# The last step of a two-part kernel, 512 tokens, is made into two steps of 256

## What is computed

```python
def _mlp(x, W1, b1, W2, b2):
    h = jax.nn.gelu(x @ W1 + b1, approximate=False)
    return h @ W2 + b2
...
def attn(x, ...):                      # x: layernorm of the input
    q, k, v = _mlp(x, W1q, ...), _mlp(x, W1k, ...), _mlp(x, W1v, ...)
    scores = jnp.einsum('bid,bjd->bij', q, k) / scale
    scores = scores * jnp.tril(jnp.ones((T, T)))
    out = jnp.einsum('bij,bjd->bid', scores, v)
    mu = jnp.mean(out, axis=-1, keepdims=True)
    var = jnp.mean(jnp.square(out - mu), axis=-1, keepdims=True)
    return (out - mu) * jax.lax.rsqrt(var + LN_EPS) * ln_w + ln_b
...
def ffn(x, tile_sigs, W, b):           # x: layernorm of the sum so far
    idx = jnp.argmax(jnp.einsum('sp,tp->st', pe, jnp.sign(tile_sigs)), axis=-1)
    y_all = jnp.einsum('bsd,tod->bsto', x, W) + b
    return the row idx[s] of y_all[b, s]
...
x = x + attn(_layernorm(x), ...)
x = x + ffn(_layernorm(x), ...)
```

## Time and profile before

| what | value |
|---|---|
| median of 3 runs | 318.12 us (317.26 to 319.13) |
| span of the profiled execution, first to last instruction | 313.3 us |
| what lies around the span, from the median | 4.8 us |
| PE busy | 288.0 us, 92% |
| DVE, ACT, POOL busy | 236.7, 188.7, 177.3 us |
| mean granted TensorE clock | 0.982 of full |

### The profile page before, as it was taken

How to read it: one execution, slowest core, us unless ns; L and a number is a source line. 1 busy time by engine, 2 the same in 40 slices (tenths; PEclk the granted TensorE clock), 3 DMA queues, 4 the chain that set the end, 5 groups by cost and what they waited for, 6 DMA issues and landing times.

```text
span 313.3 us, 5485 instructions
## 1 busy us (share of the span) xinstructions
PE 288.0 (92%) x1806; PEld 255.3 (81%) x1806; DVE 236.7 (76%) x539; ACT 188.7 (60%) x380; POOL 177.3 (57%) x238
## 2 busy tenths in 40 slices
PE   8799999998999999999999999999999975594994
PEld 6578888997898888889788989898988965583983
DVE  5858878899889979968986896798568677272556
ACT  2636677676676876676778667779664452372400
POOL 6882813360684559475646626584564857276551
PEclk9999999999999999999999999999999999599899
DMA  7909970011022110311121000250132331942111
GB/s 232 221 2 301 358 224 16 0 52 51 0 74 67 36 71 2 86 53 37 58 78 62 9 2 20 82 170 20 70 123 87 110 135 69 259 130 80 32 42 34
DMA packets 24209, 27.83 MB, mean 89 GB/s; under 512 B 4659, under 2 KB 22068, under 8 KB 24118
## 3 DMA queue, kind: packets, MB, share of 16 engines
q1 hardware_dynamic: 15910, 13.68, 15.1%
q0 software_dynamic: 3296, 8.64, 8.0%
q10 hardware_dynamic: 4976, 5.16, 5.1%
HBM read 13.95 MB, written 14.44 MB: 91 GB/s over the span
## 4 chain that ended last, share of the span: by engine, by line
PE 69%; DVE 9%; issue 6%; DMA 4%; ACT 4%; SPq 3%; POOL 2%; another core or an unknown queue 2%; ACTq 0%; POOLq 0%; DVEq 0%
PE ring L491 39%; PE o_ps L491 10%; PE s_ps L491 6%; DMA w_stage<-w2v 3%; PE w_ps L491 3%; ACT xn L982 3%; SPq L454 2%; PE ring L519 2%; PE sc_ps L604 2%; POOL out_dram L1743 1%; DVE xres L1219 1%; PE sc_ps L602 1%; PE w_ps L647 1%; DVE xres L1450 1%
## 5 line engine op out<-in xcount | busy, mean ns | idle before, releaser
L491 PE MATMUL ring<-xnT,w_sp 128*128 128x512 f32 x288 | 73.5, 399 | 5.1 <-DVE hT L1152 3.2
L491 PEld LDWEIGHTS ring<-xnT,w_sp 128*128 128x128 f32 x288 | 51.9, 189 | 17.4 <-DVE hT L1152 4.0
L882 ACT ACTIVATE ring<-ring,b_cols 128x512 f32<-128x512 f32 x48 | 31.7, 660 | 29.5 <-PE ring L491 28.2
L491 PE MATMUL ring<-hT,w_sp 128*128 128x512 f32 x192 | 46.4, 396 | 0.0
L1152 DVE TENSOR_TENSOR hT<-ring,hT 128x512 fp32r<-128x512 f32 x48 | 32.3, 680 | 14.3 <-ACT hT L885 12.7
L491 PEld LDWEIGHTS ring<-hT,w_sp 128*128 128x128 f32 x192 | 35.4, 188 | 8.1 <-DVE hT L1152 0.2
L1678 POOL DMA_INDIRECT sorted_rows<-xres,slot_i x30 | 31.2, 1041 | 8.5 <-issue 6.5
L1743 POOL DMA_INDIRECT out_dram<-slot_rows x22 | 21.9, 996 | 18.6 <-DVE slot_rows L1436 13.6
L1644 POOL TENSOR_TENSOR vtok<-v,vtok 128x512 fp32r<-128x512 f32 x14 | 17.9, 1289 | 25.4 <-ACT vtok L902 25.4
L885 ACT CAST hT<-ring 128x512 fp32r<-128x512 f32 x48 | 28.2, 587 | 1.5
L1219 DVE SCALAR_TENSOR_TENSOR xres<-cen,rs,xres 128x256 f32<-128x256 f32 x32 | 23.9, 761 | 3.6 <-issue 3.6
(11 more groups left out here) (245 smaller groups left out, 682.0 us busy)
## 6 DMA issues: line engine op xcount, KB each, us to landing
sorted_rows<-blank ACTq DMA_DIRECT2D x1, 5032.0 KB, 20.5
xt<-x SPq DMA_DIRECT2D x7, 512.0 KB, 3.6
slot_rows<-sorted_rows SPq DMA_DIRECT2D x22, 136.0 KB, 3.6
w_stage<-tile_w SPq DMA_DIRECT2D x8, 256.0 KB, 2.8
h<-sorted_rows SPq DMA_DIRECT2D x15, 136.0 KB, 3.0
xt<-x SPq DMA_DIRECT2D x2, 256.0 KB, 3.0
hT<-position_table POOLq DMA_DIRECT2D x1, 512.0 KB, 9.3
sorted_rows<-xres,slot_i POOLq DMA_INDIRECT x30
```

Of the source, the lines that this page charges most:

```text
L491: last = te.matmul(o, lhs[k][a], rhs[k][c], start=start and k == 0 and i == 0, stop=stop and k == n - 1 and i == 2, skip_group_check=check)
L882: nc.scalar.activation(full, ring[(2 + m) % 3][:, :], ACT.Gelu, bias=b1c[:, m // 2, m % 2:m % 2 + 1]).then_inc(gelu, 1)
```

## The change

Steps 0 to 6 keep 512 tokens. The former step 7 becomes step 7 (`FULL`) and step 8 (`LAST`) of 256 tokens each. Step 7 is a normal step of two chunks: it updates the state, and its back stands in the front of step 8. Step 8 holds the two dense chunks; no row of it is sorted. The sorted rows of step 7 are sent while step 8's front runs. `place(m)` moves the turning of the dense pair to position 13 (`LATER`), ahead of pair 13, and the dense products are put between pairs 13 to 17. Low parts of v are made by VectorE in both half steps, where GpSimd did it for full steps.

```diff
-STEPS = NB * PER
+FULL = NB * PER - 1
+NCH = (CH,) * FULL + (CH // 2, CH // 2)
+STEPS = len(NCH)
 LAST = STEPS - 1
+BASE = [sum(NCH[:s]) for s in range(STEPS + 1)]
...
-AMID, INNER, MIDDLE = 1, 5, 8
+AMID, INNER, MIDDLE, LATER = 1, 7, 8, 13
...
+        def place(m):
+            return m if m < LATER else LATER if m == PAIRS else m + 1
...
+            HALF_ROWS = H_ROWS + 6 * GT // ROW
...
             for n in range(H_ROWS, SLOTS):
                 if n == FIRST:
-                    sp.wait_ge(fill, FILLS * LAST + 14)
+                    rows_there(FULL)
+                if n == EARLY:
                     rows_there(LAST)
-                if n == EARLY:
-                    rows_there(STEPS)
+                if n == HALF_ROWS:
+                    sp.wait_ge(fill, FILLS * STEPS)
...
+            def last_scores():
+
+                te.wait_ge(q_lo, 2 * STEPS)
+                te.wait_ge(k_lo, 2 * STEPS)
+                te.wait_ge(xb_lo, AMID + INNER)
+                for j in range(2):
+                    mm3(sc_bank[j].rearrange("p (c n) -> p c n", n=P),
...
+            s = FULL
             front_transposes(LAST)
             back_state(s, 0)
...
+            front_h(LAST, (0, 1), False)
+            pair_transposes(3)
             back_scores(s, 0)
...
+            front_h(LAST, (2,), False)
             back_chunk(s, 1)
...
+            front_h(LAST, (3,), False)
             pair_products(3)
             pair_transposes(4)
+            front_h(LAST, (4, 5), False)
+            pair_products(4)
+            pair_transposes(5)
+            front_qk(LAST, 0, False)
+            pair_products(5)
+            pair_transposes(6)
+            front_qk(LAST, 1, False)
+            pair_products(6)
             front_v(LAST, False)
...
+            for m in range(LATER, PAIRS):
+                pair_transposes(m)
+                dense_products((m - LATER) // 4, (m - LATER) % 4)
+                pair_products(m)
+            for i in range(PAIRS - LATER, NT):
+                dense_products(i // 4, i % 4)
...
+            chunk_rest(FULL, 0)
+            chunk_rest(FULL, 1)
+            xnT_rest(LAST)
+            half_v_rest(FULL, 0)
+            half_v_rest(FULL, 1)
+            scores_rest(FULL)
+            state_rest(FULL, 0)
+            out_centred(FULL, 0)
```

More of the change, by code:

```diff
@@ L258, in mk_seq_kernel @@
         wide = carve(2 * CLASSES * NT * NJ)
+        x_late = [wide[:, i * 2 * C:i * 2 * C + 2 * C].rearrange("p (c d) -> p c d", c=2) for i in range(2)]
         chosen = wide.rearrange("p (a j t) -> p a j t", a=2 * CLASSES, t=NT)
@@ L437, in _ @@
             load_tile(1)
-            for s in range(LAST):
+            for s in range(STEPS - 3):
                 if s == 3:
@@ L551, in front_h @@
                             te.wait_ge(xnT_lo, 2 * s + 1 + k)
-                        last = mm3(ring[(2 + m) % 3][:, :], [wpair(m // 2, k, m % 2 * P, m % 2 * P + P)],
-                                   [[xnT[:, a, k, :] for a in range(2)]], start=k == 0, stop=k == KC - 1)
+                        last = mm3(ring[(2 + m) % 3][:, 0:width(s)], [wpair(m // 2, k, m % 2 * P, m % 2 * P + P)],
+                                   [[xnT[:, a, k, 0:width(s)] for a in range(2)]], start=k == 0, stop=k == KC - 1)
                     last.then_inc(fill, 1)
@@ L782, in pair_products @@
                 last.then_inc(y_ps, 1)
-            for s in range(LAST - 1):
+            for s in range(FULL - 1):
                 front_transposes(s + 1)
@@ L1101, in _ @@
             pair_norm(9)
-            for m in range(MIDDLE + 1, PAIRS + 1):
+            pair_rounded(9)
+            pair_norm(10)
+            pair_rounded(10)
+            pair_norm(11)
+            pair_rounded(11)
+            pair_norm(12)
+            pair_rounded(12)
+            pair_norm(PAIRS)
+            pair_rounded(PAIRS)
+            for m in range(LATER, PAIRS):
+                pair_norm(m)
                 pair_rounded(m)
-                if m + 1 <= PAIRS:
-                    pair_norm(m + 1)
         @block.vector
@@ L1139, in lead_var @@
                     dve.wait_ge(shift1, s - 1)
-                for c in range(CH):
+                for c in range(NCH[s]):
                     last = nc.vector.bn_aggr(mv1[:, c, :], st1[:, c, :])
@@ L1576, in _ @@
+            pair_rest(3)
+            h_rest(LAST, 2)
+            state_rest(s, 1)
+            out_centred(s, 1)
+            h_rest(LAST, 3)
+            pair_rest(4)
+            pair_out(3)
+            h_rest(LAST, 4)
+            x1_final(s, (0, 1))
+            h_rest(LAST, 5)
+            x1_stats(s)
+            pair_rest(5)
+            x1_var(s)
+            pair_out(4)
+            q_rest(LAST)
             pair_out(5)
             pair_rest(6)
+            k_rest(LAST, 0)
+            k_rest(LAST, 1)
```

729 lines of the change are left out of this document (379 added, 350 removed).

## The result

The changed kernel takes 330.33 us, median of 4 runs (327.33 to 333.60), the kernel before 318.62 (317.26 to 320.75) on the same chip. The ratio is 1.034, with an interval of 1.027 to 1.041. The changed kernel's two shortest (327.33 and 328.19) are at 1.029 of the kernel before, and five later ones at 1.038 (e9). It is slower. The forecast of 317.5 and the range up to 322 were wrong.

A forecast was written before the change was run, and what follows sets the result against it. TensorE was taken as the bound, losing 21.1 us in the tail; 205.7 + 81.2 + 2.6 + 2.1 + 8.0 + 1.9 + 3.5 + 3.5 + 4.2 = 312.7, with 4.8 around it 317.5 us; range 309 to 322.

The forecast's parts named there:

- Up to step 8's v: From the start through step 8's front: its v would end at 265.1 us.
- The joint: Between the two half steps: TensorE waits 2.1 us for v's low parts, 1.0 if `pair_norm(3)` were not in the way.
- z to `pair_products(5)`: Step 8's front: the output TensorE needs there comes 17.9 us after `back_scores(7, 0)` ends; TensorE loses 8.0 us.
- The half-wide prices: Blocks of 256 columns on ScalarE and VectorE: 0.45 us for a gelu, 0.425 for a subtraction.
- Tail, without late signals: From step 8's v to TensorE's end: 36.4 us of work plus 3.5 for slower pairs and the outputs' v.
- Late signals: Tail, beside some twenty GpSimd stores in a row: TensorE's signals come late; 3.5 us taken, between 0 and 6.3.
- The end: From TensorE's end to the span's end: 4.2 us, as in the kernel before.
- Outside the sum: Time around the span: 4.8 us, added to 312.7 to give 317.5.
- Rival (c): Tail, beside one burst of some twenty DMAs: signals late in full, 320.3 to 323 us; chance 18%.
- the 5 that would have made ScalarE the bound there: Half steps, sign of a wrong forecast: more than 5 us of small TensorE waits, and a time over 321.
- The old 6.42 us wait: Before the transposes at 269.54 in the kernel before, for sorted rows: it and its slow stretch would be gone.
- the queue: GpSimd's work ahead of `rstd_out(7)`, in step 8's front: TensorE loses 8.0 us, plus 1.9 of slow clock.

The follow-up runs named there:

- e9: The changed kernel itself measured once more, with no new edit: 327.11 us, 1.038 of the kernel before.
- e5: The changed kernel with the stores of slots 17 to 28 written by SyncE as plain DMAs, those rows missing in the output: 319.19 us, ratio 1.010.
- e4: The kernel before, with its output DMAs from slot 19 on issued when pair m + 2 is out: 318.40 us, ratio 1.012.
- e1: The changed kernel, with GpSimd's output DMAs from slot 17 on issued when pair m + 2 is out, not pair m: 325.34 us, ratio 1.032.
- e2: The changed kernel with rstd_out of step 7 moved ahead of two of four sorted chunks and two slots in GpSimd's queue: 323.17 us, ratio 1.030.
- e16: The changed kernel with rstd_out(7) moved up and slots 17 to 28 sent by GpSimd as plain DMAs, missing in the output: 322.05 us, ratio 1.022.
- e13: The changed kernel with rstd_out(7) moved up, slots 13 to 16 ahead of rstd_out(8), GpSimd operations behind slots 10, 20, 24, 28: 320.74 us, ratio 1.009.
- e14: e13 with ScalarE's pair_norm(3) moved behind the rounding of step 8's normalised tokens: 318.80 us, ratio 1.010.
- e11: The kernel before, with one GpSimd operation of about 1 us behind the stores of slots 22, 26, 30 and 34: 314.06 us, ratio 0.997.
- e10: The changed kernel with the edits of e2 and e5 together, slots 17 to 28 missing in the output: 312.45 us, ratio 0.991.
- e6: The kernel before with slots 17 to 28 written by SyncE as plain DMAs, missing in the output: 310.90 us, ratio 0.984.
- e12: The changed kernel with rstd_out(7) moved up and a GpSimd operation behind slots 20, 24, 28 and 32: 322.66 us, too wide for a ratio.
- e8: The changed kernel, rstd_out(7) moved up, slots 13 to 16 ahead of rstd_out(8), slots 19 to 28 stored one pair later: 325.22 us, ratio 1.030.

## Why the prediction was wrong

The sum was made for the span: 312.7, measured 325.5, 12.8 over. Step by step, by the traces:

- **Up to step 8's v: 265.1 taken, 266.9 measured (+1.8).** z, the end of `back_scores(7, 0)`, came at 241.7 for 239.1, since the half-wide front of step 7 loses more than the 2.6 us taken (a first wait of 2.2 alone, 227.07), and a slow clock at 228 to 231 that I had not. The joint was 2.12 for 2.1, and z to `pair_products(5)` 17.4 for 17.9: that chain was read rightly, link by link, and the wait is 5.92 for 8.0 only because TensorE came later. Here the sums of small things erred, not the mechanism. The half-wide prices held: the gelu of 256 columns has 0.450 us for my 0.45, the subtraction 0.412 for 0.425. The Trainium skill, "ScalarE: Activation LUTs", section "What ACT_TABLE_LOAD costs", gives an estimate of 0.49 for that gelu by its two figures; the measured 0.450 decides.
- **Tail, without late signals: 39.9 taken from v to TensorE's end, 43.2 measured in e5 (+3.3).** A late pair with a dense group takes 3.63 us and not 3.3 (1.73 from the dense group's start to the next products where 1.41 is the price among its like the earlier trace rows), which is 1.7 over five groups; the rest are waits of 0.2 to 0.95 us.
- **Late signals: 3.5 taken, 6.3 as the upper bound; 10.0 measured in the trace (+6.5).** This is the step that failed. From v to TensorE's end the changed kernel takes 53.2 us, e5 43.2. Of the ten, 7.05 are the one wait, 1.36 the one at 269.77, behind a remote wait of 3.34 on VectorE, and the rest is the slow clock. The prediction had the mechanism and the place. Its twenty stores in a row were four, then twelve (285.68 to 300.94), then pairs. It capped the size at two waits of about 3 us, drawn from bursts of at most eight stores. But in the longer row the signals are used later and later: 4.6, 7.0 and 8.5 us after their work's end here, 0.9, 2.3, 4.5 and 6.6 us in the row of twelve of e4. By the ratios, which don't hang on one execution, it is 7.6 to 9.0.
- **The end: 4.2 taken, 5.3 measured (+1.1)**. The stores of the last pair now end at 319.68, 0.5 us before TensorE's last block and not 2.4 before it, and the span ends 5.8 us behind them, as in e1, e2, e9 and e16.
- **Outside the sum**, 4.8 us around the span were 1.8, in my favour.

Rival (c), "late signals in full", was the right one, priced too low (320 to 323) and given 18%. Beside the joint and the queue, TensorE's waits in the half steps make 3.8 us up to 250 us, under the 5 that would have made ScalarE the bound there.

What the change is worth by its parts, in ratios to the kernel before: as it is 1.034 to 1.038; without the twelve stores 1.010; and without the long queue ahead of `rstd_out(7)` 0.991. But the kernel before without the same stores is at 0.984. The old 6.42 us wait is gone, and still no pair of runs under equal conditions shows the change to be faster. It is paid back by the queue, 5.9 us, by the rows of GpSimd's stores, which took 5.0 us before and 7.6 to 9.0 after, and by the joint, 2.1. All were in the prediction; the size of the second was not.

The edit that shortens the queue has a price of its own. In all ten traces in which `rstd_out(7)` was moved, TensorE waits before the next products into `w_ps`, from 1.72 us (e13, with a remote wait of 0.17 only beside it) to 5.15 (e16), where the changed kernel and e5 wait 0.35. So an estimate from these traces is that about 1.7 us of it comes from the order of the work, and what is over that from late signals.

A version of the change that beats the kernel before was not found with whole output: the best are e13 and e14 at 1.01. The kernel before with four pauses, e11, is level with it or a little faster (0.997).

**Still open:** why TensorE's signals are late. The runs show that indirect DMAs of GpSimd in a row do it; they don't show by what path, nor from which length on: TensorE's wait beside a row of six was 0.35 us in e5 and 5.15 in e16, and behind fours there are remote waits of 1.86 (e11) and 2.49 (e14). Also open is the 0.7% between e10 and e6, of which the joint (2.1 us) and the new wait at the row of six may be parts.

## What to carry to other kernels

When a wait in a profile is put down to no engine though the work it waits for is long done, look at what GpSimd issues at that time, and count how many indirect DMAs stand in a row, those of every kind; a cost seen beside a row of eight is no bound for a row of twelve. A change that delays GpSimd's queue makes its later stores bunch, so the price of such a row belongs in the sum of every change upstream of it. A test that takes one such row away (e10, e16) is read with a look at the other rows that are left. An edit that removes a wait should be priced with the queue of the slowest small engine ahead of the new step's first dependent, here four sorting DMAs ahead of one square root.

## What the runs showed of the hardware

- During a row of indirect DMAs by GpSimd, one each 1.28 us, signals of TensorE are used late by ScalarE and VectorE: 4.6, 7.0 and 8.5 us after the work's end in the row of twelve of the changed kernel, 2.0 us in the kernel before for work that ended between the third and the fourth store of its row of eight (at about 282.5, used at 284.45). The late releases stand 2.8 to 3.0 us apart in both kernels (297.21, 300.04 and 302.97; 284.45, 287.30 and 290.28), 3.5 to 3.6 in e2, 1.5 and 4.3 in e9. The last one comes 1 to 2 us after the row's end (302.97 after 300.94; 290.28 after 288.64; 298.42 after 296.46 in e2).
- Rows of four with an operation of 1.06 us between had no remote wait over 0.2 us in e12 and e13, but one of 1.86 in e11 and one of 2.49 in e14. Rows of six had from none (e5, 260.83 to 268.31) to waits of VectorE of 2 to 4 us (e1, e8, e13), and one of TensorE of 5.15 (e16).
- Twelve plain DMAs of the same rows, from SyncE or from GpSimd, have no remote wait beside them (e5, e16), though they move the same bytes.
- GpSimd takes 0.55 us for a plain DMA (e16's twelve in 6.5 us of GpSimd's time) and 1.28 for an indirect one, start to start.
